# Adjacency counts of a graph kernel: the key one-hots made tile by tile on VectorE

## The reference, cut to what matters

```python
neigh = x[col]                                             # col = dst
agg = jax.ops.segment_sum(neigh, row, num_segments=n)      # row = src
deg = jax.ops.segment_sum(jnp.ones((row.shape[0],), x.dtype), row, num_segments=n)
h = (x + agg / jnp.maximum(deg, 1.0)[:, None]) @ W.T + b
```

## Time and profile before

| what | value |
|---|---|
| median of 3 runs | 2717.09 us (2703.35 to 2725.47) |
| profiled execution: time | 2723.54 us |
| profiled execution: span | 2721.7 us |
| PE busy | 2125.4 us (78%) |
| DVE busy | 1428.5 us (52%) |
| ACT busy | 1246.5 us (46%) |
| mean granted TensorE clock | 0.907 |
| `adjacency`: first and last operation | 97.4 us and 409.8 us |

### The profile page before, as it was taken

The page is one execution under the profiler, slowest core; times in us unless marked ns, Lnnn a source line. Parts: engine busy times, 40 slices in busy tenths (PEclk is TensorE's granted clock), DMA queues, the critical chain, the costliest instruction groups (busy, mean ns, idle before and its releaser), DMA issues. The chain is left out here.

```text
span 2721.7 us, 46775 instructions
## 1 busy us (share of the span) xinstructions
PE 2125.4 (78%) x10923; PEld 1684.3 (62%) x10924; DVE 1428.5 (52%) x3240; ACT 1246.5 (46%) x2554; POOL 850.0 (31%) x859
## 2 busy tenths in 40 slices
PE   8678884666766766778899529749999978899996
PEld 4344442554544544555788517639999867788885
DVE  8689993666666666668434522245741535311111
ACT  3389993555555555553222313325555533222221
POOL 4300004555554555550200063535113030313233
PEclk9899996989898899989899558869999979999998
DMA  4721114555555555550100045543433343555554
GB/s 154 295 97 75 75 75 127 151 144 149 145 147 138 150 145 150 152 144 28 42 1 1 13 161 161 147 122 102 125 109 103 107 171 122 209 205 198 211 187 163
DMA packets 152022, 354.08 MB, mean 130 GB/s; under 512 B 23298, under 2 KB 106695, under 8 KB 147335
## 3 DMA queue, kind: packets, MB, share of 16 engines
q1 hardware_dynamic: 95896, 197.12, 21.6%
q0 software_dynamic: 45520, 145.80, 19.1%
q10 hardware_dynamic: 10528, 10.23, 1.1%
HBM read 275.05 MB, written 78.00 MB: 130 GB/s over the span
## 5 line engine op out<-in xcount | busy, mean ns | idle before, releaser
L949 POOL DMA_INDIRECT kv_pair<-kv,gather_idx x448 | 429.7, 959 | 384.0 <-DVE gather_idx L966 250.1
L1058 PE MATMUL p_edge_q<-QX_kept,onehot_turned 128*128 x904 | 291.6, 451 | 258.9 <-ACT onehot_turned L1021 163.7
L1058 PEld LDWEIGHTS p_edge_q<-QX_kept,onehot_turned 128*128 128x128 f32 x904 | 177.2, 213 | 358.4 <-issue 332.5
L3326 PE MATMUL ge_p<-ge_y_high,ge_counts_wide 128*128 128x256 f32 (+1 forms) x1250 | 325.7, 299 | 10.7 <-ACT ge_counts_wide L2617 6.6
L3326 PE MATMUL ge_p<-ge_y_low,ge_counts_wide 128*128 128x256 f32 (+1 forms) x1250 | 310.0, 286 | 3.5 <-issue 3.4
L1066 PE MATMUL p_sums<-R_kept 128*128 128x265 f32 x896 | 260.0, 416 | 0.0
L3326 PEld LDWEIGHTS ge_p<-ge_y_high,ge_counts_wide 128*128 128x128 f32 x1250 | 243.1, 194 | 17.7 <-ACT ge_counts_wide L2617 7.9
L3326 PEld LDWEIGHTS ge_p<-ge_y_low,ge_counts_wide 128*128 128x128 f32 x1250 | 243.6, 195 | 5.0 <-issue 3.7
L830 PE MATMUL adj_p<-adj_onehot_src,adj_onehot_key 128*128 128x416 f16 x1200 | 236.3, 348 | 10.3 <-DVE adj_onehot_src L781 5.3
L3452 PE MATMUL ge_p<-ge_y,ge_pack 128*128 128x256 f32 x928 | 215.0, 389 | 21.3 <-ACT ge_column_sums L2715 9.4
L972 DVE TENSOR_TENSOR ACC_kept<-ACC_kept,p_sums 128x265 f32 x224 | 95.9, 428 | 232.8 <-PE p_sums L1066 131.4
(11 more groups left out here) (597 smaller groups left out, 3806.3 us busy)
## 6 DMA issues: line engine op xcount, KB each, us to landing
ge_pack<-experts SPq DMA_DIRECT2D x29, 2052.0 KB
ge_counts<-adj SPq DMA_DIRECT2D x400, 104.0 KB, 2.3
adj<-adj_counts SPq DMA_DIRECT2D x100, 208.0 KB, 1.9
experts_rows<-slots_in SPq DMA_DIRECT2D x30, 256.0 KB
ge_column_sums<-slots_in SPq DMA_DIRECT2D x30, 256.0 KB
slots_out<-experts_y ACTq DMA_DIRECT2D x29, 256.0 KB
kv_pair<-kv,gather_idx POOLq DMA_INDIRECT x448
slots_in<-R_kept SPq DMA_DIRECT2D x2, 3328.0 KB, 13.2
```

The source lines that it names most:

```text
L949: pool.indirect_dma_start(kv[r][:, j, :], None, a["kv"], bass.IndirectOffsetOnAxis(ap=idx[r][:, j:j + 1], axis=0)).then_inc(kv_in[r], 16)
L1058: mm = pe.matmul(pQ[q][:, j, 0:QW], oht[q][:, j, :], QX[:, at(w), :].squeeze(1), start=True, stop=True)
L3326: mm = pe.matmul(bank[:, off:off + D], wide[parity][:, j * P:(j + 1) * P], part[:, at(m), :].squeeze(1), start=opening and off == 0 and pa ...
```

## The change

DVE no longer makes the six key one-hots in one operation (SCALAR_TENSOR_TENSOR with 32-bit inputs). It makes each by itself, in a TENSOR_SCALAR with two pointers: the first 128 columns of the 16-bit row `count`, plus the window's base, compared with the edge's key. Each stands ahead of its tile's source one-hot; the sixth, whose source one-hot is ACT's, stands last and signals a new semaphore `last_key`, for which PE waits before the last tile, beside ACT's `last_made`. All other operations are the same.

```diff
--- before.py
+++ after.py
@@ -722,6 +722,7 @@
         step, summed, far_ready = sem("step"), sem("summed"), [sem(f"far_ready{b}") for b in range(2)]
         far = [sb(f"src_distance{b}", [P, QS]) for b in range(2)]
         last_made = [sem(f"last_made{b}") for b in range(2)]
+        last_key = [sem(f"last_key{b}") for b in range(2)]
         made, used = [sem(f"made{b}") for b in range(2)], [sem(f"used{b}") for b in range(2)]
         evicted, stored, zeros_out = sem("evicted"), [sem(f"stored{b}") for b in range(TURN)], sem("zeros_out")
         mostall, bound = sb("most_all", [P, 4]), sb("bound", [P, 4])
@@ -765,8 +766,6 @@
             link = Chain(dve, step)
             for b in range(2):
                 dve.sem_inc(used[b], 1)
-            wide = [P, CHUNK, P]
-            low = C[:, C_IOTA:C_IOTA + P].unsqueeze(1).to_broadcast(wide)
 
             def window(w, b, i):
                 p = b % 2
@@ -774,10 +773,12 @@
                 with dve.Fori(0, m) as j:
                     t = nc.s_assert_within(f + CHUNK * j, 0, ETP, skip_runtime_bounds_check_because=WITHIN)
                     dve.wait_ge(used[p], v0 + j + 1)
-                    dve.scalar_tensor_tensor(out=ohk[p][:], in0=low, scalar=column(k["CF"], F_KBASE + w),
-                                             in1=key[:, at(t, CHUNK)].unsqueeze(2).to_broadcast(wide),
-                                             op0=ALU.add, op1=ALU.is_equal)
-                    for c in range(CHUNK - 1):
+                    for c in range(CHUNK):
+                        ins = dve.tensor_scalar(ohk[p][:, c, :], count[:, 0:P], column(k["CF"], F_KBASE + w),
+                                                column(key, t + c), ALU.add, ALU.is_equal)
+                        if c == CHUNK - 1:
+                            ins.then_inc(last_key[p], 1)
+                            continue
                         ins = dve.tensor_scalar(ohs[p][:, c, :], count[:], column(smod, t + c), None, ALU.is_equal)
                         if c % 2 == 0:
                             ins.then_inc(made[p], 1)
@@ -824,6 +825,7 @@
                     for n in range(CHUNK):
                         if n == CHUNK - 1:
                             pe.wait_ge(last_made[p], v0 + j + 1)
+                            pe.wait_ge(last_key[p], v0 + j + 1)
                         elif n < 2 or n == 3:
                             pe.wait_ge(made[p], (v0 + j) * (CHUNK // 2) + (n + 1) // 2 + 1)
                         for c in range(2):
```

## The result

The changed kernel takes 2764.89 us (median of 6 runs, 2757.23 to 2773.73); the kernel before, run beside it, 2718.52 us (6 runs, 2703.35 to 2725.47). The ratio is 1.0185, with a 95% interval of 1.0159 to 1.021: 46 us slower, where 40 was forecast. Its profiled execution has a span of 2771.9 us.

What follows compares the result with a forecast made beforehand. ACT was taken to bound the adjacency stage at 2.83 us a window; DVE's queue would raise it to 3.27, so 91 spacings by 0.44 us add 40 us: 2717 + 40 = 2757 us, range 2735 to 2790.

Steps and rivals of the forecast that it cites:

- What bounded the kernel: Adjacency stage after the fills: ACT sets 2.83 us a window; DVE has at most 0.17 us of slack.
- rival 3: Adjacency windows: faster, ACT's shortest spacing of 2.70 us gives back 12 us, 2705 us; chance 0.02.
- DVE's engine time: DVE in each adjacency window: six key one-hots of 0.23 us plus 1.73 make 3.11 us, against 2.66 before.
- Rival 4: DVE's key one-hots: dearer operations or addresses, 75 to 82 us more, 2792 to 2799 us; chance 0.13.
- the lower end: DVE's key one-hot at 0.18 us, as an operation with one pointer; engine time then 2.81 us a window.
- rival 2: DVE in adjacency: not slower, cheap key one-hots at four elements a cycle, ACT still sets pace, 2717 us; chance 0.10.
- DVE's queue: DVE's sequencer in each window: five added operations with addresses, 0.6 us; round 3.2 us, mean 3.27, deciding the pace.
- Rival 1: DVE in adjacency: queue hides, engine alone sets 3.11 us a window, 25 us more, 2742 us; chance 0.12.
- The turn of the outer loop: DVE's queue where its outer loop turns: 3.5 us in one window of four, against 3.2 otherwise.
- The first eight windows: Adjacency during the zero fills: cost nothing, since DVE is early and stands 10.3 us for PE.
- PE's wait for the last key: PE before a window's last tile: 3.9 us of latency across two windows, not a round, so no cost.
- rival 5: PE's matmuls in adjacency: clock falls to 1.2 GHz, 155 us more, 2872 us; chance 0.03.

Runs made afterwards that it cites:

- fixed address: Changed kernel with the key one-hots' key column no longer depending on the chunk, so five need no address: 2411.76 us, ratio 1.013 to the kernel before.
- one pointer: Changed kernel with a constant zero in place of the key one-hots' pointer to the window's base: 2763.29 us, ratio 1.0165 to the kernel before.
- one table read: Kernel before with a window's two table values packed into one, so each queue reads the table once per window: 2726.28 us, ratio 0.9987.

## Why the prediction was right

**What bounded the kernel: right, with less room than told.** "ACT sets 2.83 us" holds, but the experiment with a lighter ACT gives back 0.04 us only. That ACT waits for nobody was read from "issue" in the rows, which doesn't show it by itself, as ACT's own "issue" after the change does; the sequencer's waits in the trace bear it out. How close the others stood behind it was not in the rows. For the forecast this cost nothing, since the change went upwards; for rival 3 it means that a gain was further out of reach than its 12 us.

**DVE's engine time: right.** A key one-hot holds the engine for 0.223 us, forecast 0.23; a window 6 x 0.223 + 5 x 0.346 = 3.07 us, forecast 3.11. The fixed address shows the 3.07 as a pace. Rival 4's dear operation and the lower end (0.18) both failed; the lower end was the price of one pointer, and that one was measured at 0.163. The rows couldn't show what rival 2 says of them, that they agree with four elements a cycle. The runs do: with one pointer, 704 elements more cost 0.346 - 0.163 = 0.183 us, 0.26 ns each, a quarter of the 1.04 ns that the prediction gives for one element a cycle. What is left for the fixed cost is 0.13 us with one pointer and 0.19 with two, about twice the 75 ns that the prediction quotes, not several times.

**DVE's queue: right for the ordinary window.** 3.23 us against 3.2, by five operations with an address at 0.12 us. That it decides over the engine is shown from three sides: adding queue work alone slows the kernel, adding engine time alone leaves the window at 3.36 us, and taking either the address or a table read away shortens it. Rival 1, engine alone, would be 3.07.

**The turn of the outer loop: mis-sized.** "3.5 in one window of four" took the turn's extra 0.3 us from the kernel before. It is 3.75: 0.52 us. 0.12 us more than before is the gap behind the branch back, and 0.11 us another pause of the sequencer in the same window, between the issue of its first key one-hot and the next address. So one window of four is 0.25 us over its forecast and the others 0.03: (0.25 + 3 x 0.03)/4 is the 0.09 us by which the mean is off (3.36 - 3.27), and 91 x 0.09 = 8 us is the whole difference between 40 and the stage's 48. That the program's own 46 us came closer to 40 is within the runs' scatter, and no merit of the forecast.

**What was set at nothing: right.** The first eight windows: the first key one-hot after the fills starts at 147.1 us, 146.9 before. PE's wait for the last key: the same pace without it. PE's clock: granted 0.99 in the stage and 0.91 behind it, against 0.92, though PE's share of the stage is 76% (240 of 313.5 us) and not the 72% of rival 5, which did not occur. The stages behind start later and keep their length within a few us: the 224 products of the attention stage on DVE (L980, now L982) run from 481.9 to 1292.5 us, before from 433.8 to 1243.9, 810 us in both; L2860, now L2862, starts 54.5 us later, and the span is 50 us longer.

**What stays open.** The programs' differences in time lie between 2 us below and 11 us above what the windows of one profiled execution give: fixed address, 91 x 0.24 = 22 us in the stage and 33 us in the time; one table read, 12 us less in the stage and 8 us less in the time. No run tells where these few us go.

## What to carry to other kernels

An engine's pace has two clocks, what its operations hold and what its sequencer does between them; where a loop computes addresses and reads bounds, add up both, and compare each with the slack. Replacing one long operation by several short ones is judged on the sequencer first: each has an issue and often an address, about 0.12 us here, whatever its size. Short idle times with no releaser, in every round of a loop, are a hint that the sequencer is the bound, and no proof: here ACT and PE showed more of them than DVE, because their sequencers do their register work only behind a wait for another engine. Here the bound was the engine whose sequencer waited for nobody, and adding register work alone is the test for it.

## What the runs showed of the hardware

- **A pointer per partition costs about 0.06 us.** The same 128x128 16-bit operation holds DVE for 0.223 us with two pointers and for 0.163 with one and a constant; 32-bit input adds 0.03.
- **The turn of a loop has two prices.** 0.13 us behind the branch back when DVE executes up to 115 instructions in a turn, 0.24 to 0.27 from 134 on. The fixed address (115) and one pointer (134) lie on either side.
- **The same program ran in 2378 us in the first comparison and in 2714 to 2735 in the others.** The experiments' three comparisons ran on three chips, numbered 1, 11 and 6; whether the chip is the cause isn't shown. The adjacency stage kept its pace: the changed kernel's ordinary window is 3.23 us, and with the keys first, in that comparison, 3.21. The difference lies behind it. Here are the 224 products of the attention stage, of the kernel with queue work added, which ran in the first comparison, and of the kernel before:

```profile
L981 DVE TENSOR_TENSOR qk_prod<-kv_pair,p_edge_q x224: 690/698/706, 520.0 to 1087.3; 128x528 f32<-128x528 f32 x112
L980 DVE TENSOR_TENSOR qk_prod<-kv_pair,p_edge_q x224: 690/698/706, 433.8 to 1243.9; 128x528 f32<-128x528 f32 x112
```

  The same products take 567 us in place of 810, each as long as before, so the time lies between them. From 560 to 1080 us, where both are in this stage, the granted clock is 1.00 in the one and 0.91 in the other, and the DMA engines move 210 GB/s against 146. Ratios of different comparisons are therefore not to be set side by side to the last tenth of a per cent; the windows of the stage are. Why the attention stage runs faster there wasn't pursued.
